# Score matmuls of two duos in one burst, over a ring of six PSUM banks

## The reference

```python
x = x + tanh(g_xattn) * attention(layernorm(x), ctx, mask)   # q = ln(x) Wq, k = ctx Wk, v = ctx Wv, softmax over keys, Wo
x = x + tanh(g_ffn) * sum_e w_e * (silu(y W1_e) * (y W2_e)) W3_e   # y = layernorm(x), w = softmax of the top 2 of y Wg
```

## Time and profile before

| | us |
|---|---|
| median of 3 runs | 699.1 (698.22, 699.1, 701.25) |
| the profiled execution | 698.08 |
| its span in the trace | 696.3 |
| attention steps on TensorE | from 32.9 to about 406 |
| experts | from 468 to the end |

### The profile page before, as it was taken

How to read it: one execution, slowest core, us unless ns; L and a number is a source line. 1 busy time by engine, 2 the same in 40 slices (tenths; PEclk the granted TensorE clock), 3 DMA queues, 4 the chain that set the end, 5 groups by cost and what they waited for, 6 DMA issues and landing times.

```text
span 696.3 us, 10945 instructions
## 1 busy us (share of the span) xinstructions
PE 628.6 (90%) x2958; PEld 349.6 (50%) x2959; DVE 389.6 (56%) x1161; ACT 285.3 (41%) x742; POOL 309.1 (44%) x272
## 2 busy tenths in 40 slices
PE   4599999999999999999999994419999999999995
PEld 2344455454555444555545542405566666666663
DVE  3676988888978879887799753221122222222221
ACT  2456755565555555645465520102222222222221
POOL 2344655555555885646856452240233222222221
PEclk9899999999999999999999999558999999999998
DMA  8805776768674867565877683969332222222222
GB/s 278 297 1 121 172 162 142 173 140 176 141 155 107 189 167 177 125 155 129 204 153 173 124 194 110 373 192 353 90 60 45 45 45 45 45 44 46 45 45 35
DMA packets 92643, 95.25 MB, mean 137 GB/s; under 512 B 11056, under 2 KB 86704, under 8 KB 92592
## 3 DMA queue, kind: packets, MB, share of 16 engines
q1 hardware_dynamic: 69872, 71.54, 40.6%
q10 hardware_dynamic: 15936, 14.17, 8.9%
q0 software_dynamic: 6784, 8.95, 8.0%
HBM read 27.72 MB, written 12.36 MB: 58 GB/s over the span
## 4 chain that ended last, share of the span: by engine, by line
PE 69%; POOL 7%; SPq 6%; DMA 6%; DVE 5%; issue 4%; ACT 1%; ACTq 0%; POOLq 0%; DVEq 0%
PE ps_s L1313 14%; PE ps_s L1134 13%; PE ps_o L1159 13%; PE ps_o L1339 7%; PE ps_a L1169 7%; PE ps_a L1066 7%; POOL x_regrouped L459 3%; POOL probs L471 3%; DMA out_dram<-yg,ids 2%; PE ps_o L1145 2%; DMA wg_sb<-WgT_dram 2%; PE ps_t L1332 2%; DVE blocksT L880 2%; PE ps_a L1104 1%; DMA xg<-x_regrouped 1%
## 5 line engine op out<-in xcount | busy, mean ns | idle before, releaser
L471 POOL TENSOR_TENSOR probs<-probs,inv_sum 128x802 f32<-128x802 f32 x128 | 194.8, 1523 | 154.2 <-DVE inv_sum L859 153.4
L584 ACT ACTIVATE probs<-probs,neg_max 128x401 f32<-128x401 f32 x256 | 159.2, 624 | 146.8 <-DVE neg_max L868 146.7
L868 DVE CUSTOM_DVE_ANT_0 probs<-ps_s,biases 128x401 f32<-128x401 f32 x256 | 136.9, 572 | 52.6 <-PE ps_s L1134 52.1
L1313 PE MATMUL ps_s<-w_sb,xgT 128*128 x296 | 141.9, 603 | 1.4 <-ACT xgT L684 1.4
L880 DVE STREAM_TRANSPOSE blocksT<-probs 128x832 f32<-128x832 f32 x128 | 133.1, 1040 | 9.0 <-POOL probs L471 9.0
L518 POOL DMA_INDIRECT out_dram<-yg,ids x36 | 55.9, 1552 | 171.7 <-DVE yg L1030 128.3
L1159 PE MATMUL ps_o<-probsT,v_sb 128*64 128x512 f32 x512 | 123.8, 606 | 3.5 <-DMA probsT<-blocksT 3.5
L1134 PE MATMUL ps_s<-kT,qT 64*128 64x201 f32 (+1 forms) x1024 | 121.9, 357 | 1.4 <-DMA wg_sb<-WgT_dram 1.4
L1134 PEld LDWEIGHTS ps_s<-kT,qT 64*128 64x128 f32 x1024 | 82.8, 187 | 78.9 <-DVE neg_max L868 42.2
L1018 DVE TENSOR_TENSOR gated<-ps_s,silu 128x512 f32<-128x512 f32 x37 | 25.6, 692 | 136.3 <-PE ps_s L1313 136.3
L1313 PEld LDWEIGHTS ps_s<-w_sb,xgT 128*128 128x128 f32 x296 | 54.1, 194 | 41.6 <-issue 39.9
(11 more groups left out here) (127 smaller groups left out, 421.9 us busy)
## 6 DMA issues: line engine op xcount, KB each, us to landing
probsT<-blocksT SPq DMA_DIRECT2D x288, 96.0 KB
probsT<-blocksT SPq DMA_DIRECT2D x96, 128.0 KB
probsT<-blocksT ACTq DMA_DIRECT2D x96, 96.0 KB
xg<-x_regrouped SPq DMA_DIRECT2D x39, 129.0 KB, 2.1
probsT<-blocksT ACTq DMA_DIRECT2D x32, 128.0 KB
w_sb<-W1T_dram SPq DMA_DIRECT2D x8, 512.0 KB, 8.3
w_sb<-W2T_dram SPq DMA_DIRECT2D x8, 512.0 KB, 8.6
w_sb<-W3T_dram SPq DMA_DIRECT2D x8, 512.0 KB, 10.7
```

Source lines behind the costliest of these rows:

```text
L471: pool.tensor_tensor(duo, duo, inv_sum[:, u:u + 2].unsqueeze(2).to_broadcast([P, 2, LASTK]), ALU.mult)\
L584: act.activation(probs[:, b, 0:LASTK], probs[:, b, 0:LASTK], ACT.Exp, bias=neg_max[:, b:b + 1], scale=-1.0, accum_out=sum_exp[:, b:b + 1]) ...
L868: dve.tensor_tensor_reduce(probs[:, b, 0:LASTK], ps_s[u % 4][:, 0:LASTK], biases[:, tile, :], HD ** -0.5, 3e38, ALU.add, ALU.min, neg_max[ ...
L1313: mm = pe.matmul(bank[:, :], xgT[:, buf, k, :], w[:, k, bass.ds(expert, 1), :].squeeze(1), start=(k == 0), stop=(k == KT - 1))
```

## The change

Three things go together. In every even step TensorE now does `scores(n)` and `scores(n + 1)` one after the other, and none in odd steps. The two transpose banks join the score banks in a ring of six, `ps_ring`: duo d writes to banks 2d and 2d+1 modulo 6 and waits for VectorE's read of duo d-3. And since `ps_t` now holds scores, the six late transposes of x (calls 2 to 7) go to `ps_o` and `ps_a` in turn, with waits until V and the queries have left these banks, and `queries(3)` (step 9) and the first `probs_v` (step 11) wait for the copies of the transposes. VectorE, ScalarE, GpSimd and SyncE keep their order.

```diff
+        ps_ring = ps_s + ps_t
...
+        def xn_bank(c):
+            return ps_t[c] if c < 2 else [ps_o, ps_a][c % 2]
...
-                act.copy(xnT[:, c % 2, c // 2 * GQ:(c // 2 + 1) * GQ], ps_t[c % 2][:, :]).then_inc(xnT_ready, 1)
+                act.copy(xnT[:, c % 2, c // 2 * GQ:(c // 2 + 1) * GQ], xn_bank(c)[:, :]).then_inc(xnT_ready, 1)
...
-                        dve.tensor_tensor_reduce(probs[:, b, 0:LASTK], ps_s[u % 4][:, 0:LASTK], biases[:, tile, :],
+                        dve.tensor_tensor_reduce(probs[:, b, 0:LASTK], ps_ring[u % 6][:, 0:LASTK], biases[:, tile, :],
...
-                    mm = pe.transpose(ps_t[c % 2][:, t * P:(t + 1) * P], tile[:, k * P:(k + 1) * P], ident[:, :])
+                    mm = pe.transpose(xn_bank(c)[:, t * P:(t + 1) * P], tile[:, k * P:(k + 1) * P], ident[:, :])
...
-                    if d >= 2:
-                        pe.wait_ge(masked_ready, 2 * d - 2)
+                    if d >= 3:
+                        pe.wait_ge(masked_ready, 2 * d - 4)
...
-                            mm = pe.matmul(ps_s[(2 * d + odd) % 4][:, k0:k1], qT[h0:h0 + HD, c % 2, t * P:(t + 1) * P],
+                            mm = pe.matmul(ps_ring[(2 * d + odd) % 6][:, k0:k1], qT[h0:h0 + HD, c % 2, t * P:(t + 1) * P],
...
+                            pe.wait_ge(xnT_ready, 2 * NR)
...
-                    if n < DUOS:
+                    if n % 2 == 0 and n < DUOS:
                         scores(n)
+                        scores(n + 1)
...
                     if 2 * NS <= n < 2 * NS + 3:
+                        pe.wait_ge(v_ready, 2 * NS)
+                        pe.wait_ge(q_ready, (n + 2) // 4 + 1)
...
-                        if n // 4 + 1 == HP:
+                        if n == 2 * NS + 1:
+                            pe.wait_ge(xnT_ready, 6)
+                        if n // 4 + 1 == 4:
                             pe.wait_ge(xnT_ready, 2 * NR)
```

## The result

| | before | after |
|---|---|---|
| median of 20 runs | 699.17 (696.72 to 702.39) | 702.02 (699.25 to 705.09) |
| span of the profiled execution | 696.3 | 700.9 |
| first scores to VectorE's last read of scores | 372.36 | 374.33 |

The ratio of the runs is 1.0033, with a 95% interval of 1.0019 to 1.0046: slower by a third of a per cent, inside what the prediction called the same. The time forecast was 700.8.

The account below looks back on a forecast made before the run. TensorE was taken to bound the kernel, busy in 90% of the span. Terms -11.0 + 1.9 + 4.1 + 2.9 + 0.8 + 2.7 + 0.3 = +1.7 gave 699.8 us profiled, 700.8 for runs; range 694 to 707.5.

Parts of the forecast that it names:

- 55 pairs: Steps 12 and 13 and chunks 4 to 30: each pair of duos nets 0.20 us, together -11.0.
- V, and steps 8 to 11: Start: V matmuls wait for copies in steps 0 to 7, +1.9; transposes, queries and `probs_v` wait in 8 to 11, +4.1.
- router copies: Queries wait for router transposes at steps 57, 89, 121 and for counts at 65, 97: +2.9 us.
- statistics lag: Router statistics use up the 0.8 us cover of the `qT` copy by some 0.25 once a group: +0.8 us.
- scatter, waits for `qT`: In GpSimd's four scatter steps a group, projections stall 0.65 and 2.0 us for `qT`; net of today's stalls +2.7.
- clock in the attention: Rival: stalls in steps 9 to 11 and scatter stretches halve TensorE's clock, 1.7 us a fall; two give 704.2; chance 0.18.
- the unseen boundary: Projection to `probs_v`, absent from the earlier trace: taken to cost 0.2 us; if this one were free, the time is 695.3.
- The cover of 0.8: Chunk: ScalarE's copy of `qT` ends at 6.1 us, the projection needs it at 6.9; called the tightest cover.
- The tail: After the attention: repeats as before, with +0.3 us added for a later last mask.
- Boundaries are free: Rival: the new order's boundaries cost nothing, 55 pairs save 0.2 us more, time 690; chance 0.12.
- The pair is no pair: Rival: the second duo's wait opens the boundary, all 11.0 us go, time 711.8; chance 0.04.
- VectorE and ScalarE can't follow in twos: Rival: cover gone in about 19 chunks with router steps, their 0.40 us each is lost, time 708.4; chance 0.14.

Follow-up runs that it names:

- Experiment 2: Changed kernel with pairs only in steps 0 to 10, single duos over the six banks from step 12 on; 707.01 us, ratio 1.009 to before.
- experiment 1: Changed kernel with steps 0 to 11 as before the change, pairs over six banks from step 12 on; 697.92 us, ratio 0.9955 to before.
- experiment 3: Changed kernel with the router's second transposes ahead of `probs_v` and their copy ahead of the output copy; 702.71 us, ratio 1.0029 to before.
- experiment 4: Changed kernel with one scatter in each of eight steps instead of two in each of four; 696.41 us, ratio 0.9932 to before.
- experiment 5: Kernel before the change with one scatter in each of eight steps instead of two in each of four; 697.69 us, ratio 0.9961 to before.
- experiment 6: Changed kernel with old steps 0 to 11, pairs from step 12 on, and one scatter a step; 689.83 us, ratio 0.9852 to before.

## Why the prediction was right, and where it was right by luck

The time, 702.0, lies in the range, and the direction of the small difference is that of the sum. Its terms, in the order of the prediction:

| term | predicted | measured |
|---|---|---|
| 55 pairs | -11.0 | -0.40 a chunk, so -11.0 |
| V, and steps 8 to 11 | +6.0 | +5.66; 5.2 by the means of all eight traces |
| router copies | +2.9 | +3.2, of which 3.0 are idle time |
| statistics lag | +0.8 | +0.5 |
| scatter, waits for `qT` | +2.7 | +2.0 |
| clock in the attention | 0, a rival | +1.65 |
| sum at the last read | +1.4 | +1.97 |

The measured column compares the two traces chunk by chunk, from start to start, with an undisturbed chunk of 11.10 and 10.70; so it holds the short delays as well, and leaves nothing over but rounding.

**The pairs.** The saving of 0.20 came out to the hundredth, and so did the decision on the unseen boundary: projection to `probs_v` costs as much as projection to scores (1.92 against the 1.93 derived from the earlier trace rows). Taking the nearest row, and not nothing, is what kept the forecast from the 695.3 of that rival. The distance to before falls from +5.47 at duo 16 to +2.68 at duo 44, seven chunks, 0.40 each. Experiment 2 shows that the order alone does it, not the banks. The prediction calls the 0.2 the price of "one boundary" and also of "going in and out". It is that of one boundary: a distance from start to start holds just one, and a chunk with eight boundaries before and six after got shorter by 0.40. That it is the shape of the matmuls that costs is not shown by a run of its own. For it speaks that the second duo of a pair also has other operands and other banks, and adds only 1.56 - 0.88 = 0.68 us.

**The start.** 6.0 was forecast and 5.66 measured: 2.2 against 1.9 in steps 0 to 7, 3.5 against 4.1 in steps 8 to 11. The waits are 3 x 0.73 + 0.81 for V (0.8 each forecast), 0.89 and 1.47 around the transposes, 1.91 in front of `probs_v`. Experiments 1 and 2 put 5.2 and 5.5 on steps 0 to 11 from the two sides. This is the largest part of what ate the gain, and it is not a cost of bursts: it is the cost of starting them while V and the transposes still share banks with something else.

**The router.** 3 x 0.75 + 2 x 0.33 = 2.9 forecast, 2.3 + 0.7 = 3.0 of idle time measured, and 3 x 0.81 + 2 x 0.41 = 3.2 in the lengths of the chunks. The mechanism was right; that it can't be had back by a change of order alone (experiment 3) the prediction had not asked.

**The scatter.** The mechanism was right, the size was not. The prediction had two stalls a group, 0.65 and 2.0. The second is there, 2.17 both times, but of the first only 0.20 and 0.08 are left. From start to start the two groups lose 4.75 in all, and 2.77 before: a rise of 2.0, not 2.7. Experiments 4 and 5 confirm the place from both kernels.

**The statistics lag.** The cover of 0.8 measured 0.87, and the 0.25 once a group came out as 0.23 and 0.24, but in two groups of three: in the middle one, which in the change comes right behind the scatter's stall and the fall of the clock, there is none, while experiment 1, without the fall, has 0.09 and 0.16 there too. So it is 0.5 and not 0.8. The place and the chain (VectorE's maximum, ScalarE's exponentials, the copy of `qT`) are in the rows; no run took the statistics away.

**The clock.** It was a rival with a chance of 0.18, "two falls give 704.2". One fall came in the attention of the profiled execution, behind the first of the two 2.17 stalls, and cost 1.65; in steps 9 to 11, where the rival looked for one as well, none came. Against this and the router's 0.3 too little stand the scatter's 0.7, the start's 0.3 and the lag's 0.3 too much, and in so far the sum is good by luck. One fall shows in the profile of the change and, at the same place, in that of experiment 3, and none in those of experiments 1, 2, 4, 5 and 6; each of these is one execution.

**The tail.** +0.3 was forecast. From the last read to the end of the span it is +1.4 in this trace, and TensorE shows 1.7 of it: the last `probs_v`, once more behind a wait of 3.8 for its blocks, was run at half the clock, 5.35 us for what takes 3.65:

```profile
424.46 5.35 PE L1164 MATMUL ps_o<-probsT,v_sb 128*64 128x512 f32 x16 [3.77 <-DMA probsT<-blocksT]
```

I don't count this to the change. Over the eight traces the tail varies by 4 us without following any edit: 290.4 in experiment 6, 291.0 before, 292.4 here, 294.4 in experiment 4. What decides it stays open.

**The rivals.** "Boundaries are free" (690) is refuted by the chunk of 10.70. "The pair is no pair" is refuted by 1.56. "VectorE and ScalarE can't follow in twos" is refuted in the steady part, where TensorE has no gap; beside the 0.24 at the statistics it was true behind the scatter alone, and there GpSimd is the cause.

## What to carry to other kernels

Regrouping matmuls so that groups of different shape meet less often paid here exactly the number of boundaries that went, so count those that the new order creates as well: each pair removed two and made one, and 0.20 us was left. Before shortening a step, list what the work between two users of one bank was hiding (copies of V, of transposes, of the router), and what else runs at a pace close to the step's; start the new order only where these are through, and spread what bursts. The sum of such stalls was as large as the gain, and two local edits, a later start of the bursts and a spread scatter, turned +0.3% into -1.5%.

## What the runs showed of the hardware that was not expected

- The clock does not answer to a single stall alone. Six stalls of 2.16 or 2.17 us in front of a projection stand in the traces of the change and of experiments 1 and 3, two in each. Behind two of them, the first of the change and the first of experiment 3, the granted clock fell to half, for 3.4 us; behind the other four, one of them in the change itself at 358.34, it stayed at full. Experiment 1 has nearly the same one at the same place, 2.16 us ahead of a projection between a full burst and a full `probs_v`, and the projection then takes its usual time from start to start, 259.75 - 257.82 = 1.93; in the change, behind 2.17, it takes 2.68. Timeline of TensorE in experiment 1:

```profile
254.03 1.63 PE L1146 MATMUL ps_s<-kT,qT 64*128 64x201 f32 x16
257.82 1.99 PE L1181 MATMUL ps_a<-wo_sb,oT 128*128 128x256 f32 x8 [2.16 <-ACT qT L549]
259.75 1.94 PE L1171 MATMUL ps_o<-probsT,v_sb 128*64 128x512 f32 x8
```

  What else decides, one profile of each can't tell.
- A boundary between two matmul groups of different shape costs about 0.2 us each, whichever of these shapes meet: 64-row scores next to 128-row work, and 128-column projections next to the 64-column `probs_v`, with the durations from start to start unchanged at 1.87 and 1.92. The tail of the change has both halves of `probs_v` one behind the other, with no boundary between them. They take 418.69 - 415.11 = 3.58 instead of 2 x 1.87 = 3.74, so one boundary there is worth 0.16:

```profile
415.11 3.65 PE L1164 MATMUL ps_o<-probsT,v_sb 128*64 128x512 f32 x16
418.69 1.99 PE L1174 MATMUL ps_a<-wo_sb,oT 128*128 128x256 f32 x8
```

- An indirect transfer holds GpSimd for some 1.2 us (2.71 for a scaling and one, 1.53 of it the scaling; 4.00 with two). So two in a step of 2.67 make it the slowest engine of that step, though it is busy for only 44% of the span.
